# A graph network layer: own rows recomputed in the step loop instead of stored in phase 1, and two parts of a step reordered

## The chip, the cores and the metric

The kernel runs on one core of a Trainium2 chip. The metric is the device time of one execution in microseconds. The engines are PE (TensorE matmuls; PEld its weight loads), DVE (VectorE), ACT (ScalarE), POOL (GpSimd) and SP (SyncE, which here only issues DMAs). Each works through its own list of instructions in order; they meet at semaphores.

## The reference

```python
h = jnp.maximum(_layernorm(x, axis=-1), 0.0)          # x: 6250 x 128
src_h = h[src]                                        # 206250 edges, sorted by dst
parts = [relu(h)]
for t in range(3):
    msg = relu(src_h @ W_e[t].T + b_e[t])             # masked to edge_type == t
    parts.append(segment_sum(msg, dst, num_segments=N))
agg = concatenate(parts, axis=1)                      # 6250 x 512
for t in range(3):
    updated = where(node_type == t, agg @ W_n[t].T + b_n[t], updated)
x = x + updated + h
```

## The kernel before

Nodes stand in 49 blocks of 128 (`NB`). **Phase 1** makes a table of messages in DRAM: for each block ACT normalises x to h (`norm`, L680), PE transposes h (`tr`, L500), ACT copies hT out of PSUM (`copy_t`, L688), PE multiplies hT with the edge weights (`mm`, L506 and L508), ACT or DVE applies relu, and SP stores the rows. Besides, SP stores each hT to `own_hT` (L368), POOL adds h to x in place (L448), and SP stores that in four parts to `own_x` (L372). DVE works on the edges' indices meanwhile.

**The step loop** has 271 steps (`STEPS`). The sorted edges are 403 groups of 512. The first 265 groups (`NS`) are gathered one in each step: POOL fetches message rows by four indirect DMAs (L457), DVE makes a one-hot (`hot`, L973), PE multiplies (`gathered`, L561), DVE adds the sums into `acc` (`add`, L985). The other 138 groups go through counts: they form 23 batches (`BATCHES`) of 6 groups, taken once for each of three edge types, so 69 in all (index q). For each group and type there is a build (`count`, L575): DVE makes two kinds of one-hots (`dense_hot`, L1001 and L1003, at most three sets ahead), PE multiplies them, ACT copies the counts out (`counted`, L743). Seven products (`product`, L589) multiply a batch's counts with message planes held in SBUF. Builds and products are the pieces of a step, three or four, dealt out evenly by `pieces(s)`. A batch ends so: if its last product is in step LAST, then DVE sums three parts in step LAST+1 (`dense_sum`, L1018), PE transposes the slots in LAST+2 (`turn_slots`, L596), and DVE adds six windows into `acc` in LAST+3 (`dense_add`, also L985). The first product of batch q waits for the adds of batch q-2 (L585), because they read the PSUM bank it writes. When the message planes change type, at steps 0 to 3, 86 to 89 and 171 to 175, ACT and DVE split new planes (L752, L754, L1025, L1027).

A node block whose edges are all in is finished (`fin_at`, 49 of them, at least two steps apart and closer together towards the end): SP has loaded `own_x` to `xr` and `own_hT` to SBUF, PE runs L605, L606 (with hT) and L608 into PSUM bank `psF`, DVE adds the masked result to `xr` by three operations (L1036), and SP stores.

DVE's order in a step is: `hot` of the next step, `add`, `dense_add`, `finish`, `dense_hot` for the next step's builds, splits, `dense_sum`. PE's is: `gathered`, `finish`, all pieces, `turn_slots`. ACT's is `counted`, then splits.

Of the kernel before, what the change touches and what calls it, by code (L numbers as in the profile page):

```python
# [4 lines left out]
F32 = mybir.dt.float32  # L5
# [7 lines left out]
P = 128  # L13
# [28 lines left out]
def build(nc, x, src, dst, etype, ntype, w_e, b_e, w_n, b_n, out):  # L42
# [25 lines left out]

    own_x = nc.dram_tensor("own_x", [NB * P, D], F32, kind="Internal").ap()
    own_hT = nc.dram_tensor("own_hT", [NB, D, P], F32, kind="Internal").ap()  # L70
# [68 lines left out]
    with ExitStack() as ctx:  # L139
# [81 lines left out]
        hT_own = work[:, 4 * TD + 4 * D:4 * TD + 8 * D].rearrange("p (s d) -> p s d", s=4)  # L221
        fb_h_own = work[:, 0:D]
        fb_hT_own = work[:, D:2 * D]
# [66 lines left out]
        xh_ok = sem("xh_ok")  # L290
        xh_out = sem("xh_out")
        hT_out = [sem(f"hT_out{i}") for i in range(UN)]
        hT_ld = [sem(f"hT_ld{i}") for i in range(4)]
# [32 lines left out]
        KEPT = (0, 13, 26, 38, NB)  # L326
# [19 lines left out]
        def _(sp):  # L346
# [19 lines left out]
            for i in range(NB):  # L366
                sp.wait_ge(hT_ok, i + 1)
                sp.dma_start(own_hT[i, :, :], hT[:, i % UN, :]).then_inc(hT_out[i % UN], 16)  # L368
                if i + 1 in KEPT:
                    a = KEPT[KEPT.index(i + 1) - 1]  # L370
                    sp.wait_ge(xh_ok, i + 1)
                    sp.dma_start(own_x[a * P:(i + 1) * P, :].rearrange("(b p) d -> p b d", p=P),  # L372
                                 xb[:, a * D:(i + 1) * D].rearrange("p (b d) -> p b d", d=D)).then_inc(xh_out, 16)
                sp.wait_ge(tab_msg[i % UN], i // UN + 1)
                n = min(P, N - i * P)
                sp.dma_start(table[i * P:i * P + n, :], msg[0:n, i % UN, :]).then_inc(tab_out[i % UN], 16)

            for s in range(UN):
                sp.wait_ge(hT_out[s], 16 * len(range(s, NB, UN)))
            sp.wait_ge(xh_out, 16 * (len(KEPT) - 1))  # L380
# [16 lines left out]
            def load_x(j):  # L397
# [4 lines left out]
                sp.dma_start(xr[0:n, j % 4, :], own_x[i * P:i * P + n, :]).then_inc(x_ld[j % 4], 16)  # L402
                sp.dma_start(hT_own[:, j % 4, :], own_hT[i, :, :]).then_inc(hT_ld[j % 4], 16)
# [22 lines left out]
        def _(pool):  # L426
# [18 lines left out]

            for i in range(NB):
                pool.wait_ge(h_ok, i + 1)
                pool.tensor_tensor(xb[:, blk(i)], xb[:, blk(i)], h[:, i % UN, :], ALU.add).then_inc(xh_ok, 1)  # L448
# [34 lines left out]
        def _(pe):  # L483
# [114 lines left out]

            def finish(j):
                i = ORDER[j]  # L600
                pe.wait_ge(hT_ld[j % 4], 16 * (j // 4 + 1))
                if j >= 1:
                    pe.wait_ge(fin_ok, j)
                pe.wait_ge(acc_add, THROUGH[READY[i]])
                pe.matmul(psF[:, 0:TD], ones[:, :], bn_3[:, :], start=True, stop=False)  # L605
                pe.matmul(psF[:, 0:TD], hT_own[:, j % 4, :], wnT[:, 0, :], start=False, stop=False)  # L606
# [7 lines left out]
            for s in range(STEPS):  # L614
                if s < NS:
                    gathered(s)
                for j in fin_at(s - 1):
                    finish(j)
                for kind, i in pieces(s)[:1]:
                    if kind == "build":  # L620
                        count(i)
                    else:
                        product(i)
                for kind, i in pieces(s)[1:]:
# [4 lines left out]
                for q in turns_of(s):  # L629
                    turn_slots(q)  # L630

            rest = pe.value_load(flag[0:1, 0:1], min_val=0, max_val=1)
            with pe.If(rest > 0):
# [11 lines left out]
                with pe.Fori(0, NB) as i:  # L645
                    pe.wait_ge(fb_h, i + 1)
                    pe.transpose(psF[:, TD:TD + P], fb_h_own, ident[:, :]).then_inc(fb_t, 1)
                    pe.wait_ge(fb_hT, i + 1)
                    pe.matmul(psF[:, 0:TD], ones[:, :], bn_3[:, :], start=True, stop=False)
                    pe.matmul(psF[:, 0:TD], fb_hT_own, wnT[:, 0, :], start=False, stop=False)  # L650
# [6 lines left out]
        def _(act):  # L657
# [19 lines left out]
            def norm(i):  # L677
                if i >= UN:
                    act.wait_ge(xh_ok, i - UN + 1)
# [3 lines left out]
            def copy_t(i):  # L683
                act.wait_ge(h_t, i + 1)
                if i >= 4:
                    act.wait_ge(tab_mm, i - 3)
                    act.wait_ge(hT_out[i % UN], 16 * (i // UN))
# [67 lines left out]

            act.wait_ge(xh_out, 16 * (len(KEPT) - 1))
            for s in range(STEPS):
# [377 lines left out]
```

## Time and profile before

| | us |
|---|---|
| three runs | 1755.31, 1756.76, 1765.67 (median 1756.76) |
| the profiled execution, one of the three | 1765.67 |
| its span in the trace | 1763.8 |

In the page, times are microseconds, a line like L589 is line 589 of the kernel, and a group's row gives the mean duration of one instruction and what ended the idle time before it. "issue" as a releaser means that the trace names none on the engine's own side, "remote" one that it does not know. Matmul ends are modelled. Busy time over the span is PE 1514.6 us (86%), DVE 1042.6 (59%), ACT 547.2 (31%), POOL 1163.0 (66%).

### The profile page before, as it was taken

Reading aid. Unit: us, or ns where it says so; the run is one execution under the profiler, and the core shown is the slowest. Engines: PE = TensorE matmul, PEld = TensorE weight load, DVE = VectorE, ACT = ScalarE, POOL = GpSimd, SP = SyncE. Lnnn points to the kernel's source line nnn. Section 1 sums busy time; section 2 is a strip of 40 time slices with the busy share of each in tenths; the row PEclk is TensorE's granted clock in tenths of the full one; section 3 lists DMA queues with packets and bytes.
Section 4 is the critical chain, followed back from the end, with each engine's and each line's share of the span. In section 5 each row is a group of like instructions: output and inputs, shape, how many; then the busy total and the mean of one; then the engine's idle time right before and its main releaser. Section 6 shows DMA issues by size and latency. Waiting matters only on the chain.

```text
span 1763.8 us, 27736 instructions
## 1 busy us (share of the span) xinstructions
PE 1514.6 (86%) x9585; PEld 1191.5 (68%) x9585; DVE 1042.6 (59%) x3461; ACT 547.2 (31%) x1031; POOL 1163.0 (66%) x1125
## 2 busy tenths in 40 slices
PE   6956888988899887889888888887889898989997
PEld 2445677767677676767676777676767777777774
DVE  8565565565656567556555565558556556565642
ACT  7552232322232334322222232234222222223210
POOL 4467666666767676676676677766776666666660
PEclk9868889989999988988988999989999998999998
DMA  8642111111111123111111111213112222122220
GB/s 281 210 123 65 42 48 50 47 49 49 50 49 49 46 68 94 48 49 49 46 47 49 49 47 49 71 47 88 49 50 53 53 53 53 53 58 53 55 54 25
DMA packets 99382, 113.26 MB, mean 64 GB/s; under 512 B 21526, under 2 KB 79413, under 8 KB 99243
## 3 DMA queue, kind: packets, MB, share of 16 engines
q0 software_dynamic: 33920, 69.54, 15.1%
q1 hardware_dynamic: 64445, 40.93, 7.6%
q8 instruction: 78, 1.28, 0.3%
q10 hardware_dynamic: 878, 1.02, 0.2%
q14 instruction: 61, 0.50, 0.1%
HBM read 92.17 MB, written 19.22 MB: 63 GB/s over the span
## 4 chain that ended last, share of the span: by engine, by line
PE 56%; DVE 18%; issue 10%; another core or an unknown queue 10%; ACT 3%; DVEq 2%; DMA 1%; ACTq 0%; SPq 0%
PE ps L589 22%; PE ps L575 13%; PE ps L561 9%; DVE arena L1001 7%; PE ps L608 5%; DVE lhot L1003 4%; DVE acc L985 3%; PE ps L508 2%; PE ps L606 2%; ACT mem L754 1%; DVE xr L1036 1%; DVEq L985 1%; DVE onehot L973 1%; DVE work L1025 1%
## 5 line engine op out<-in xcount | busy, mean ns | idle before, releaser
L457 POOL DMA_INDIRECT rows<-message_table,idx x1060 | 1125.0, 1061 | 515.8 <-issue 284.0
L743 ACT CAST arena<-ps 128x500 f16<-128x500 f32 x828 | 443.0, 581 | 1074.2 <-PE ps L575 636.5
L589 PE MATMUL ps<-mem,arena 128*120 128x384 bf16 x3381 | 698.2, 350 | 42.6 <-issue 35.1
L589 PEld LDWEIGHTS ps<-mem,arena 128*120 128x120 f16 x3381 | 469.6, 145 | 176.2 <-issue 72.0
L575 PE MATMUL ps<-arena,lhot 128*128 128x200 bf16 x3312 | 447.2, 284 | 112.9 <-issue 75.1
L985 DVE TENSOR_TENSOR acc<-ps,acc 128x20 f32 (+1 forms) x679 | 131.7, 194 | 571.3 <-remote 331.0
L1001 DVE TENSOR_SCALAR arena<-iota_j,jkey 128x400 bf16<-128x400 f16 (+1 forms) x1656 | 457.5, 337 | 8.4 <-remote 8.2
L575 PEld LDWEIGHTS ps<-arena,lhot 128*128 128x128 bf16 x3312 | 335.9, 109 | 181.4 <-issue 111.4
L561 PEld LDWEIGHTS ps<-onehot,rows 128*128 128x128 f32 x2120 | 281.5, 202 | 74.1 <-issue 68.6
L561 PE MATMUL ps<-onehot,rows 128*128 128x27 f32 x2120 | 277.4, 270 | 59.4 <-issue 34.3
L1003 DVE TENSOR_TENSOR lhot<-iota_l,lkey 128x512 bf16<-128x512 f16 x414 | 281.2, 679 | 0.0
L608 PE MATMUL ps<-wnT,acc 128*128 128x384 f32 x294 | 117.4, 541 | 0.0
L1036 DVE SCALAR_TENSOR_TENSOR xr<-ps,mask,xr 128x128 f32<-128x128 f32 x147 | 51.5, 351 | 84.1 <-PE ps L608 57.3
L608 PEld LDWEIGHTS ps<-wnT,acc 128*128 128x128 f32 x294 | 62.9, 214 | 47.5 <-issue 15.3
L973 DVE TENSOR_TENSOR onehot<-iota_w,key 128x108 f32<-128x108 f32 x265 | 68.4, 258 | 0.0
L448 POOL TENSOR_TENSOR arena<-arena,work 128x128 f32<-128x128 f32 x49 | 34.3, 710 | 46.3 <-ACT work L680 45.8
L508 PE MATMUL ps<-weT,work 128*128 128x384 f32 x98 | 50.5, 601 | 2.6 <-ACT work L688 2.6
L606 PE MATMUL ps<-wnT,work 128*128 128x384 f32 x98 | 49.5, 590 | 0.3 <-issue 0.3
L1018 DVE TENSOR_REDUCE slots<-ps 120x128 f32<-120x384 f32 x69 | 37.7, 546 | 0.0
L1027 DVE TENSOR_TENSOR mem<-work,mem 128x896 bf16<-128x896 f32 x21 | 22.9, 1092 | 21.1 <-ACT mem L754 19.1
L754 ACT CAST mem<-work 128x896 bf16<-128x896 f32 x21 | 19.7, 938 | 45.9 <-DVE work L1025 29.9
L596 PE MATMUL ps<-ident,slots 120*128 120x120 f32 x69 | 19.2, 279 | 7.6 <-DVE slots L1018 6.5
(105 smaller groups left out, 335.8 us busy)
## 6 DMA issues: line engine op xcount, KB each, us to landing
rows<-message_table,idx POOLq DMA_INDIRECT x1060
message_table<-work SPq DMA_DIRECT2D x48, 192.0 KB, 1.9
work<-message_table SPq DMA_DIRECT2D x18, 448.0 KB
own_hT<-work SPq DMA_DIRECT2D x49, 64.0 KB, 1.7
work<-own_hT SPq DMA_DIRECT2D x49, 64.0 KB
xr<-own_x SPq DMA_DIRECT2D x48, 64.0 KB
out_dram<-xr SPq DMA_DIRECT2D x48, 64.0 KB
own_x<-arena SPq DMA_DIRECT2D x2, 832.0 KB, 4.2
```

What stands on the lines that cost most here:

```text
L457: pool.indirect_dma_start(out=rows[:, g % SLOTS, u, :], out_offset=None, in_=table_rows, in_offset=bass.IndirectOffsetOnAxis(ap=idx[:, g, ...
L508: pe.matmul(psH[s][:, 0:TD], hT[:, s, :], weT[:, :], start=False, stop=True).then_inc(tab_mm, 1)
L561: m = pe.matmul(to[:, :, OFF[u]:OFF[u] + WS], rows[:, s % SLOTS, u, :], onehot[:, s % 4, u, :].rearrange("p (t w) -> p t w", t=T), start=( ...
L575: t = pe.matmul(to[:, :, OFF[u]:OFF[u] + WID[u]], lhot[:, i % HOTS, u, 0:P], jhot[:, i % HOTS, a:a + HH * WID[u]], start=(u == 0), stop=(u ...
L589: m = pe.matmul(psQ[q % 2][0:BG * WG, 0:3 * D], counts[q % 2][:, c * MC + e, :], planes[:, c * MC + e, :, :].rearrange("p v d -> p (v d)") ...
L606: pe.matmul(psF[:, 0:TD], hT_own[:, j % 4, :], wnT[:, 0, :], start=False, stop=False)
L608: m = pe.matmul(psF[:, 0:TD], nodes[:, t, i * P:(i + 1) * P], wnT[:, 1 + t, :], start=False, stop=(t == T - 1))
L743: act.copy(counts[q % 2][:, half * HH:(half + 1) * HH, k * WG:(k + 1) * WG], psB[m % 4][:, 0:HH * WG].rearrange("p (h w) -> p h w", w=WG)) ...
L973: dve.tensor_tensor(onehot[:, s % 4, :, :], iota_b, key[:, s, :].unsqueeze(2).to_broadcast(shape), ALU.is_equal).then_inc(hot_ok, 1)
L985: dve.tensor_tensor(there, sums_, there, ALU.add).then_inc(acc_add, 1)
L1001: dve.tensor_scalar(jhot[:, i % HOTS, JAT[u]:JAT[u] + HB * w], iota_j[w][:, :], float(t * HB * w), jkey[:, g, u:u + 1], ALU.add, ALU.is_equal)
L1003: dve.tensor_tensor(lhot[:, i % HOTS, :, :], iota_l[:, :].unsqueeze(1).to_broadcast([P, TPG, P]), lkey[:, g, :].unsqueeze(2).to_broadcast( ...
```

## The change

- The DRAM buffers `own_x` and `own_hT`, their stores by SP, the add on POOL and all waits for them go.
- In the loop SP loads x itself to `xr`. At the end of the step before a block's step s = FIN, ACT computes h from it (`own_norm`). In step s PE transposes it after the gathered group and ahead of the pieces (`own_transpose`), ACT copies it out of PSUM as the first thing of the step (`own_copy`), and DVE adds h to `xr` (`own`) before `finish` and the one-hots. The block's matmuls follow in step s + 1 as before.
- `turn_slots` moves on PE from the end of a step to behind its first piece.
- `dense_add` moves on DVE from behind `add` to the end of the step.

The core of the diff (left out: the semaphores' names, the views of `work`, and the part that runs only when edges do not fit the plan, which does not happen here):

```diff
@@ sync
             for i in range(NB):
-                sp.wait_ge(hT_ok, i + 1)
-                sp.dma_start(own_hT[i, :, :], hT[:, i % UN, :]).then_inc(hT_out[i % UN], 16)
-                if i + 1 in KEPT:
-                    a = KEPT[KEPT.index(i + 1) - 1]
-                    sp.wait_ge(xh_ok, i + 1)
-                    sp.dma_start(own_x[a * P:(i + 1) * P, :].rearrange("(b p) d -> p b d", p=P),
-                                 xb[:, a * D:(i + 1) * D].rearrange("p (b d) -> p b d", d=D)).then_inc(xh_out, 16)
                 sp.wait_ge(tab_msg[i % UN], i // UN + 1)
...
-            for s in range(UN):
-                sp.wait_ge(hT_out[s], 16 * len(range(s, NB, UN)))
-            sp.wait_ge(xh_out, 16 * (len(KEPT) - 1))
...
-                sp.dma_start(xr[0:n, j % 4, :], own_x[i * P:i * P + n, :]).then_inc(x_ld[j % 4], 16)
-                sp.dma_start(hT_own[:, j % 4, :], own_hT[i, :, :]).then_inc(hT_ld[j % 4], 16)
+                sp.dma_start(xr[0:n, j % 4, :], x[i * P:i * P + n, :]).then_inc(x_ld[j % 4], 16)
@@ gpsimd
-            for i in range(NB):
-                pool.wait_ge(h_ok, i + 1)
-                pool.tensor_tensor(xb[:, blk(i)], xb[:, blk(i)], h[:, i % UN, :], ALU.add).then_inc(xh_ok, 1)
@@ tensor
+            def own_transpose(j):
+                pe.wait_ge(own_h, j + 1)
+                if j >= 1:
+                    pe.wait_ge(fin_ok, j)
+                pe.transpose(psF[:, TD:TD + P], h_own[:, j % 2, :], ident[:, :]).then_inc(own_t, 1)
+
             def finish(j):
                 i = ORDER[j]
-                pe.wait_ge(hT_ld[j % 4], 16 * (j // 4 + 1))
-                if j >= 1:
-                    pe.wait_ge(fin_ok, j)
+                pe.wait_ge(own_st, j + 1)
                 pe.wait_ge(acc_add, THROUGH[READY[i]])
...
-                pe.matmul(psF[:, 0:TD], hT_own[:, j % 4, :], wnT[:, 0, :], start=False, stop=False)
+                pe.matmul(psF[:, 0:TD], hT_own[:, j % 2, :], wnT[:, 0, :], start=False, stop=False)
...
                     finish(j)
+                for j in fin_at(s):
+                    own_transpose(j)
                 for kind, i in pieces(s)[:1]:
                     if kind == "build":
                         count(i)
                     else:
                         product(i)
+                for q in turns_of(s):
+                    turn_slots(q)
                 for kind, i in pieces(s)[1:]:
                     if kind == "build":
                         count(i)
                     else:
                         product(i)
-                for q in turns_of(s):
-                    turn_slots(q)
@@ scalar
             def norm(i):
-                if i >= UN:
-                    act.wait_ge(xh_ok, i - UN + 1)
...
                     act.wait_ge(tab_mm, i - 3)
-                    act.wait_ge(hT_out[i % UN], 16 * (i // UN))
...
-            act.wait_ge(xh_out, 16 * (len(KEPT) - 1))
+            def own_norm(j):
+                i = ORDER[j]
+                act.wait_ge(x_ld[j % 4], 16 * (j // 4 + 1))
+                if j >= 2:
+                    act.wait_ge(own_t, j - 1)
+                    act.wait_ge(own_add, j - 1)
+                act.activation(h_own[:, j % 2, :], xr[:, j % 4, :], ACT.Relu, scale=rstd[:, i:i + 1],
+                               bias=nbias[:, i:i + 1]).then_inc(own_h, 1)
+
+            def own_copy(j):
+                act.wait_ge(own_t, j + 1)
+                if j >= 2:
+                    act.wait_ge(fin_mm, j - 1)
+                act.copy(hT_own[:, j % 2, :], psF[:, TD:TD + P]).then_inc(own_st, 1)
+
             for s in range(STEPS):
+                for j in fin_at(s):
+                    own_copy(j)
                 for kind, i in pieces(s):
                     if kind == "build":
                         counted(i)
                 for m in splits_at(s):
                     split(m)
+                for j in fin_at(s + 1):
+                    own_norm(j)
@@ vector
+            def own(j):
+                dve.wait_ge(own_h, j + 1)
+                dve.tensor_tensor(xr[:, j % 4, :], xr[:, j % 4, :], h_own[:, j % 2, :], ALU.add).then_inc(own_add, 1)
...
-                dve.wait_ge(x_ld[j % 4], 16 * (j // 4 + 1))
+                dve.wait_ge(own_add, j + 1)
...
-            dve.wait_ge(xh_out, 16 * (len(KEPT) - 1))
...
-                for q in adds_of(s):
-                    dense_add(q)
+                for j in fin_at(s):
+                    own(j)
                 for j in fin_at(s - 1):
                     finish(j)
...
                 for q in sums_of(s):
                     dense_sum(q)
+                for q in adds_of(s):
+                    dense_add(q)
```

## Rows read from the trace of the kernel before

**Rows 1.** Page, part 2: TensorE clock in 40 slices, tenths of full speed.

```profile
PEclk9868889989999988988988999989999998999998
```

**Rows 2.** Windows view, three stages: length, busy us (instructions) of PE, PEld, DVE, ACT, POOL, clock.

```profile
0.00:105.00 105.00, 80.78 (x262) 36.69 (x262) 71.54 (x189) 67.61 (x162) 44.70 (x72) 0.92 0.69 228
...
195.00:1715.00 1520.00, 1338.37 (x8839) 1083.31 (x8839) 906.91 (x3084) 448.01 (x818) 1043.85 (x987) 0.92 0.20 53
1715.00:1764.00 49.00, 37.18 (x139) 23.58 (x137) 11.51 (x45) 0.00 (x0) 7.54 (x8) 0.82 0.10 27
```

**Rows 3.** Waits view, 195 to 1715 us: total us, times, longest us.

```profile
DVE acc L985 <- remote: 317.6, 93, 9.4
...
PE ps L575 <- issue: 71.2, 97, 3.2
...
PE ps L575 <- DVE lhot L1003: 25.8, 22, 3.3
```

**Rows 4.** Timeline of 800 to 809 us, DVE, then PE: start, length.

```profile
801.90 0.22 DVE L985 TENSOR_TENSOR acc<-ps,acc 128x60 f32 x1 [1.05 <-PE ps L561]
802.78 0.83 DVE L985 TENSOR_TENSOR acc<-ps,acc 128x20 f32 x3 [0.65 <-issue]
...
804.86 1.12 DVE L1001 TENSOR_SCALAR arena<-iota_j,jkey 128x400 bf16<-128x400 f16 x4
805.90 0.68 DVE L1003 TENSOR_TENSOR lhot<-iota_l,lkey 128x512 bf16<-128x512 f16 x1
...
807.56 0.68 DVE L1003 TENSOR_TENSOR lhot<-iota_l,lkey 128x512 bf16<-128x512 f16 x1
...
804.61 0.97 PE L561 MATMUL ps<-onehot,rows 128*128 128x27 f32 x8
806.64 0.98 PE L575 MATMUL ps<-arena,lhot 128*128 128x200 bf16 x8 [1.06 <-DVE lhot L1003]
807.45 1.15 PE L589 MATMUL ps<-mem,arena 128*120 128x384 bf16 x6
```

**Rows 5.** Timeline: slots' sum and PE's second piece, first and last case.

```profile
245.79 0.55 DVE L1018 TENSOR_REDUCE slots<-ps 120x128 f32<-120x384 f32 x1
...
245.40 1.31 PE L589 MATMUL ps<-mem,arena 128*120 128x384 bf16 x7
...
1625.16 0.55 DVE L1018 TENSOR_REDUCE slots<-ps 120x128 f32<-120x384 f32 x1
...
1625.23 2.13 PE L589 MATMUL ps<-mem,arena 128*120 128x384 bf16 x7
```

**Rows 6.** Groups by line, whole run: busy us, mean ns | idle before, releasers.

```profile
L680 ACT ACTIVATE work<-arena,nbias,rstd 128x128 f32<-128x128 f32 x49 | 23.8, 488 | 0.0
...
L596 PE MATMUL ps<-ident,slots 120*128 120x120 f32 x69 | 19.2, 279 | 7.6 <-DVE slots L1018 6.5 <-issue 1.0
...
L500 PE MATMUL ps<-ident,work 128*128 128x128 f32 x49 | 14.9, 307 | 0.8 <-ACT work L680 0.8
L688 ACT COPY work<-ps 128x128 f32<-128x128 f32 x49 | 12.7, 260 | 7.9 <-DMA own_hT<-work 4.3 <-PE ps L500 2.8 <-PE ps L508 0.7
```

**Rows 7.** Chain that ended last, 54 to 72 us: start, us, what.

```profile
54.74 3.79 DMA own_hT<-work
...
60.23 1.58 PE ps L508 x2
...
62.46 1.58 PE ps L508 x2
...
69.12 1.50 PE ps L508 x2
70.62 0.11 PE ps L500
...
71.00 0.84 PE ps L508 x2
```

**Rows 8.** Timeline of the last two blocks, PE and DVE.

```profile
1753.00 0.32 PE L605 MATMUL ps<-bn,ones 3*128 3x384 bf16 x1 [1.33 <-issue]
...
1757.43 0.32 PE L605 MATMUL ps<-bn,ones 3*128 3x384 bf16 x1 [1.33 <-issue]
...
1756.20 1.12 DVE L1036 SCALAR_TENSOR_TENSOR xr<-ps,mask,xr 128x128 f32<-128x128 f32 x3 [3.30 <-PE ps L608]
```

More of the change, by code:

```diff
@@ L67, in build @@
     table_rows = table.rearrange("n (t d) -> (n t) d", t=T)
-    own_x = nc.dram_tensor("own_x", [NB * P, D], F32, kind="Internal").ap()
-    own_hT = nc.dram_tensor("own_hT", [NB, D, P], F32, kind="Internal").ap()
     D0, D1 = 1, NS - 8
@@ L220, in build @@
         st = [work[:, a * MC * D:(a + 1) * MC * D].rearrange("p (h d) -> p h d", h=MC) for a in range(2)]
-        hT_own = work[:, 4 * TD + 4 * D:4 * TD + 8 * D].rearrange("p (s d) -> p s d", s=4)
-        fb_h_own = work[:, 0:D]
-        fb_hT_own = work[:, D:2 * D]
+        h_own = work[:, 4 * TD + 4 * D:4 * TD + 6 * D].rearrange("p (s d) -> p s d", s=2)
+        hT_own = work[:, 4 * TD + 6 * D:4 * TD + 8 * D].rearrange("p (s d) -> p s d", s=2)
         xr = sb("xr", [P, 4, D])
@@ L289, in build @@
         o_st = [sem(f"o_st{i}") for i in range(4)]
[L290 to L293, printed above, removed]
+        own_h = sem("own_h")
+        own_add = sem("own_add")
+        own_t = sem("own_t")
+        own_st = sem("own_st")
         fin_mm = sem("fin_mm")
@@ L325, in build @@
         SETS = "AAADDDADAD"
-        KEPT = (0, 13, 26, 38, NB)
         EDGE_LOADS = 3 * (GB + 1) + 1
@@ L618, in _ @@
                     finish(j)
+                for j in fin_at(s):
+                    own_transpose(j)
                 for kind, i in pieces(s)[:1]:
[L620 to L624, printed above, removed]
                     if kind == "build":
@@ L630, in _ @@
                     turn_slots(q)
+                for kind, i in pieces(s)[1:]:
+                    if kind == "build":
+                        count(i)
+                    else:
+                        product(i)
             rest = pe.value_load(flag[0:1, 0:1], min_val=0, max_val=1)
@@ L646, in _ @@
                     pe.wait_ge(fb_h, i + 1)
-                    pe.transpose(psF[:, TD:TD + P], fb_h_own, ident[:, :]).then_inc(fb_t, 1)
+                    pe.transpose(psF[:, TD:TD + P], h_own[:, 0, :], ident[:, :]).then_inc(fb_t, 1)
                     pe.wait_ge(fb_hT, i + 1)
                     pe.matmul(psF[:, 0:TD], ones[:, :], bn_3[:, :], start=True, stop=False)
-                    pe.matmul(psF[:, 0:TD], fb_hT_own, wnT[:, 0, :], start=False, stop=False)
+                    pe.matmul(psF[:, 0:TD], hT_own[:, 0, :], wnT[:, 0, :], start=False, stop=False)
                     for t in range(T):
@@ L787, in again @@
                     act.wait_ge(fb_x, i * 16 + 16)
-                    act.activation(fb_h_own, xr[:, 0, :], ACT.Relu, scale=rstd[:, bass.ds(i, 1)],
+                    act.activation(h_own[:, 0, :], xr[:, 0, :], ACT.Relu, scale=rstd[:, bass.ds(i, 1)],
                                    bias=nbias[:, bass.ds(i, 1)]).then_inc(fb_h, 1)
@@ L791, in again @@
                     act.wait_ge(fb_t, i + 1)
-                    act.copy(fb_hT_own, psF[:, TD:TD + P]).then_inc(fb_hT, 1)
+                    act.copy(hT_own[:, 0, :], psF[:, TD:TD + P]).then_inc(fb_hT, 1)
                     act.wait_ge(fb_row, i + 2)
@@ L1103, in _ @@
                     dve.wait_ge(fb_h, i + 1)
-                    dve.tensor_tensor(xr[:, 0, :], xr[:, 0, :], fb_h_own, ALU.add).then_inc(fb_xh, 1)
+                    dve.tensor_tensor(xr[:, 0, :], xr[:, 0, :], h_own[:, 0, :], ALU.add).then_inc(fb_xh, 1)
                     dve.wait_ge(fb_xh, i + 1)
```

## The prediction

> **What bounds the kernel now.** I read the page's clock line first, then the busy time by stage, then who waits for whom inside the long stage, then single stretches in order of time, and last the chain in the first stage and the end. The stages [rows 2] show where the time is: 105 us of preparation, then the step loop, 1520 us of it between 195 and 1715, then 49 us of tail. In the loop PE is busy 1338 of 1520 us, DVE 907, ACT 448, POOL 1044: PE sets the pace, and what can be won or lost is its idle time (182 us), its amount of work, and its clock. The granted clock is 0.92 on the mean there [rows 2]; it goes up and down between slices [rows 1], so some stretches run at the lower of the two levels (1.2 instead of 2.4 GHz), and each hole in PE's work can buy another one.
>
> The waits of the loop [rows 3] say what the holes are: before a build matmul (L575) PE waits 25.8 us, 22 times, for DVE's one-hots (L1003), and 71.2 us over which the trace names no releaser. DVE in turn waits 317.6 us before its add (L985) with an unnamed releaser. So the two engines hand a step back and forth, and the place of DVE's dense add in a step matters, as does every wait that is put in PE's queue.
>
> **Phase 1: the copies of own x and hT go.** PE's chain per tile is two L508, one L500, one L506. At 54.7 us the chain runs over the DMA of own_hT for 3.79 us, and then PE's pair takes 1.58 us instead of 0.84, from 60.23 to 69.12 us, five tiles at the lower clock [rows 7]. Without these 53 stores the table's stores (three times the bytes of hT's) have the DMA queues to themselves. ACT's wait for these stores is 4.3 us in all [rows 6], of which I take 2.5, and I take the slow stretch as its consequence: five tiles at 2.23 us (62.46 less 60.23 is such a distance; the chain's rows are a tile apart) against 1.21 us, 5 x 1.0 = 5.0 us. Sum -7.5 us; bounds 0 (DVE's edge preparation is late by itself) and -9.3 us. The adds on POOL (L448) stand nowhere in that chain; taking them away is worth nothing. SP's queue only becomes shorter.
>
> **The dense add moves behind the one-hots.** In the step at 801 us [rows 4] DVE adds the gathered sums at 801.90, then the six dense adds run from 802.78 to 804.86, and only then come the one-hots of the next step: the first set is ready at 806.58. PE's gathered group ends at 805.59 (804.61 + 0.98), and it waits 1.06 us. With the dense adds last, the first set would be ready about 2.8 us earlier, and this wait goes. But 0.8 us later, at 807.45, PE starts the first product of a batch, and this product waits for the dense adds of the batch before the last (acc_add). In the new order they end where now the second one-hot ends, 807.56 + 0.68 = 808.24: the product starts 0.8 us later than now. The wait is exchanged, not removed. By the plan in the code, 48 of the 67 such products fall into the step right after a dense add; in 18 of them only one piece is ahead, and in 10 two pieces with two sets of one-hots in DVE's way. So up to 28 x 0.8 = 22 us are lost; PE often arrives later than in this row, so I take half, +10. The gain is at most all that [rows 3] name, 25.8, and a part of the unnamed 71.2; it is kept where no product is gated in that step. I take -18: of the 25.8 about half, and 5 us of the unnamed. Net -8 us, bounds -61 (all the named, half the unnamed, no loss) and +22.
>
> **The turn of a batch's slots moves ahead.** PE's L596 needs DVE's sum (L1018). Now it stands last in its step, and waits three times, 6.5 us in all [rows 6]. In the new place it comes after one piece. In the rows, the sum ends at 246.34 where PE passes that place at 245.40, and at 1625.71 against 1625.23 [rows 5]; these are the first and the last of 28 cases (of 68) in which the sum is later, by 30 us together, three of them (the steps of the split planes, 15 us) with a wait already there. While PE waits for the turn, the pieces behind it stand, and with them the next gathered group. But PE's records may run ahead of what it has finished (the unnamed waits of DVE), and then the turn costs nothing. Bounds 0 and +30; I take the middle, +16 us.
>
> **Own h is computed in the loop.** 49 transposes of 128x128 are added to PE. The same form takes 307 ns (L500) and 279 ns (L596) by itself [rows 6], and in a full queue the next matmul starts 0.11 us on, the length of L500 in the chain [rows 7]. 49 x 0.11 = 5.4 to 49 x 0.31 = 15 us; taken 10. TensorE: Matmul & The Clock Gate of the Trainium skill (Part 4, PE-mode transpose) gives about 275 ns for such a transpose inside a kernel; by the page the sum would be 49 x 0.275 = 13.5 us instead of 10, and the forecast 3.5 us higher. The transposes wait for ACT's norm (L680, 488 ns), issued after ACT's copies of the step before; PE has the gathered group (0.98 us) as cover. A copy of a build just ended and the norm are longer than that by 0.1 to 0.5 us where the step ends with a build. Queued behind the waiting transpose are PE's pieces. Bounds 0 and 49 x 0.49 = 24 us; taken +5. ACT's copy (260 ns) and norm are work for an engine that is busy 448 of 1520 us. DVE's added 49 adds of 128x128 have no row; between 0.19 and 0.35 us each they lie in its idle time. SP's load of hT goes, and x is loaded from the input: no change.
>
> **Tail.** At the end a block takes 4.43 us (1753.00 to 1757.43): PE's matmuls, then three DVE operations, and PE starts 0.11 us after DVE ends (1756.20 + 1.12 against 1757.43) [rows 8]. The transpose of a block waits for the end of the block before, so 0.31 + 0.26 + two handovers of 0.1 come on top: 0.75 us x 6 blocks = +4 us; bounds 0 and +6.
>
> **Clock.** More short holes in PE cost clock. I add +3 us (three stretches like that of [rows 7], 1 us each); bounds 0 and +30: at 0.90 instead of 0.92 the 1338 us of PE's work become 1338 x 0.92/0.90 = 1368.
>
> **Sum.** -7.5 - 8 + 16 + 10 + 5 + 4 + 3 = +22.5 us on a span of 1763.8. The profiled execution took 1765.67 us in its own timing, the slowest of the three, the median is 1756.76; 22.5/1765.67 = 1.3%, so 1779 us against the median.
>
> **Rivals.**
> *The new waits are hidden.* PE's finished work lags behind its records, so that turn and norm are there in time: 0 for both, 5 for the transposes, no clock term. -7.5 - 8 + 5 + 4 = -6.5 us: 1750 us. For it: DVE's 317.6 us of unnamed waits [rows 3]; against it: where PE runs without holes (244 to 248 us), the turn's data are late by the records [rows 5].
> *The other side: DVE's order was the main brake.* If the unnamed waits before L575 are in truth late one-hots, half of them goes with the named: -61 + 10 for the gated products, -9 in phase 1, +5 turn, +5, +4: -46 us, 1711 us. It decides the sign of the case as soon as some 40 us of L575's 97 us of idle vanish. Against it: the exchange in [rows 4], and that the new order delays the dense adds for the next products.
> *The clock falls.* The transposes and holes push the granted clock of the loop to 0.90: +22.5 - 3 + 30 = +49.5 us, 1806 us. For it: 0.82 in the tail, where PE's work has such holes already [rows 2].
>
> **How the numbers follow.** Forecast 0.42, hidden waits 0.32, other side 0.14, clock 0.12. About 1% (17.6 us) is what a measurement of this kernel can tell from no change. The forecast's own range is 1764 to 1797, so some of it falls within 1%: slower by over 1% 0.48, within 1% 0.38, faster by over 1% 0.14. The range reaches to the hidden case and a little below it (1743) and up to the clock case (1810), leaving out the other side and the far end of the clock.
>
> **What would show it.** Right: PE's first gathered group some 7 us earlier; L575's wait for L1003 under 12 us; a new wait of L589 for DVE's add of about 10 us; L596's wait for L1018 15 us or more over some 25 places; a tail 4 us longer. Wrong: L596's wait still about 6 us and no wait before the new transposes (hidden case); PE's idle time in the loop down by 40 us (other side); a clock of 0.90 or less, or one above 0.93, in the loop.

## The result, and the profile after

The changed kernel takes 1806.16 us (median of four, 1801.04 to 1811.46) where the kernel before takes 1756.03 (four, 1751.76 to 1765.67): ratio 1.0277, 95% interval [1.0226, 1.0331], slower by about 49 us (1756.03 x 0.0277). Ratios, here and below, leave out executions that took over 1.5% longer than the fastest of the same kernel (three of ten of one kernel below, and one of the kernel before). 1779 us were predicted, with 1743 to 1810 as the range. The direction and the range hold; the size doesn't: +1.3% was forecast, +2.8% came.

The profiled execution took 1800.96 us, 35.3 more than that of before (1765.67, the slowest of its four). Lines have moved: `gathered` is L541 now, `count` L555, `product` L569, `turn_slots` L576, the new transpose L583, PE's `finish` L589 to L592, ACT's `counted` L726, `own_norm` L745, `own_copy` L752, DVE's `add` and `dense_add` L986, the one-hots L1002 and L1004, `dense_sum` L1019, `own` L1032, `finish` L1041.

The page's busy line and clock line of the changed kernel, to be held against [rows 1]:

```profile
PE 1524.0 (85%) x9634; PEld 1201.8 (67%) x9634; DVE 1050.5 (58%) x3510; ACT 579.9 (32%) x1129; POOL 1127.5 (63%) x1076
...
PEclk9977889899989888989888998988899899999997
```

PE is busy 1524.0 us where it was 1514.6: 9.4 us more. The span is 35.1 us longer (1798.9 against 1763.8), so 25.7 us are new idle time of PE. In these two executions most of the cost is waits, not PE's added work.

The windows view, same stages as [rows 2] (the tail is shifted by the 35 us):

```profile
0.00:105.00 105.00, 84.56 (x262) 37.55 (x262) 66.77 (x186) 65.09 (x161) 9.57 (x22) 1.00 0.46 161
195.00:1715.00 1520.00, 1314.10 (x8726) 1069.26 (x8724) 906.11 (x3090) 470.60 (x891) 1025.24 (x970) 0.91 0.19 51
1750.00:1799.00 49.00, 35.97 (x109) 21.31 (x109) 11.93 (x48) 3.56 (x11) 3.38 (x4) 0.74 0.07 18
```

In the same 1520 us of the loop PE gets through 8726 matmuls instead of 8839 and stands idle 206 us instead of 182. The granted clock is 0.91 instead of 0.92. The first stage reads 1.00 (0.92 before) and holds exactly as many matmuls, 262; these two clock figures are too high, as the part on phase 1 shows.

The waits view from 195 to 1715 us (columns as in [rows 3]):

```profile
DVE acc L986 <- remote: 284.6, 93, 7.9
...
PE ps L569 <- issue: 54.1, 80, 8.1
...
PE ps L583 <- ACT work L745: 45.3, 17, 5.3
...
PE ps L555 <- issue: 29.1, 59, 1.4
...
PE ps L576 <- DVE slots L1019: 23.4, 17, 6.5
...
PE ps L569 <- DVE acc L986: 10.2, 10, 2.0
...
PE ps L555 <- DVE lhot L1004: 1.5, 4, 0.6
```

The wait for the one-hots, 25.8 us in [rows 3], is down to 1.5. The turn's wait (L576) has gone from 6.5 us in [rows 6] to 23.4, and the gated product (L569 for L986) has appeared with 10.2. Of the named waits of PE the largest is the one I had costed at 5 us: the new transpose waits 45.3 us, 17 times, for ACT's norm. One of these waits in the timeline of the changed kernel (start, length, engine, line; idle before in brackets):

```profile
1449.43 0.98 PE L541 MATMUL ps<-onehot,rows 128*128 128x27 f32 x8
...
1453.66 1.05 ACT L726 CAST arena<-ps 128x500 f16<-128x500 f32 x2 [2.38 <-remote]
1454.00 0.22 DVE L986 TENSOR_TENSOR acc<-ps,acc 128x60 f32 x1 [2.68 <-remote]
1454.60 0.51 ACT L745 ACTIVATE work<-xr,nbias,rstd 128x128 f32<-128x128 f32 x1
...
1455.16 0.47 PE L583 MATMUL ps<-ident,work 128*128 128x128 f32 x1 [4.75 <-ACT work L745]
```

PE's gathered group ends at 1450.41 by its record, but DVE can add its sums only at 1454.00, and ACT gets the last build of the step before only at 1453.66. (A build's counts come out in two copies.) Behind these two copies stands the norm (1454.60), and behind the norm PE. So of the 4.75 us named, PE has lost about the 1.16 us after 1454.00, and the handover to DVE just before it; earlier its own work wasn't finished. Perfetto Trace Analysis of the Trainium skill (Tensor Engine Instruction) says that a matmul's end in a profile is estimated, not observed. The trace agrees: 3.59 us lie between the recorded end, 1450.41, and the first use of the result, 1454.00.

### The profile page after: what moved, and what is told of

It is laid out like the page before. It is cut to its first block, busy times and chain, and to the rows that moved or that the text cites. A ratio compares the mean times of both kernels' runs of the same rounds, so it can differ in the third digit from the quotient of the medians.

```text
span 1798.9 us, 27966 instructions
## 1 busy us (share of the span) xinstructions
PE 1524.0 (85%) x9634; PEld 1201.8 (67%) x9634; DVE 1050.5 (58%) x3510; ACT 579.9 (32%) x1129; POOL 1127.5 (63%) x1076
## 4 chain that ended last, share of the span: by engine, by line
PE 60%; DVE 14%; issue 11%; another core or an unknown queue 9%; ACT 4%; DVEq 1%; ACTq 0%
PE ps L569 24%; PE ps L555 15%; PE ps L541 8%; DVE arena L1002 5%; PE ps L592 4%; DVE lhot L1004 3%; PE ps L488 3%; DVE acc L986 2%; PE ps L590 2%; ACT arena L726 2%; DVE xr L1041 1%; DVE work L1026 1%; ACT mem L737 1%; PE ps L486 1%
## 5 line engine op out<-in xcount | busy, mean ns | idle before, releaser
L726 ACT CAST arena<-ps 128x500 f16<-128x500 f32 x828 | 446.0, 580 | 1010.4 <-PE ps L555 552.4
L569 PE MATMUL ps<-mem,arena 128*120 128x384 bf16 x3381 | 702.3, 351 | 69.7 <-issue 55.5
L569 PEld LDWEIGHTS ps<-mem,arena 128*120 128x120 f16 x3381 | 472.7, 145 | 200.4 <-issue 98.2
L555 PE MATMUL ps<-arena,lhot 128*128 128x200 bf16 x3312 | 452.4, 288 | 45.9 <-issue 32.2
L1002 DVE TENSOR_SCALAR arena<-iota_j,jkey 128x400 bf16<-128x400 f16 (+1 forms) x1656 | 460.8, 339 | 4.9 <-remote 4.8
L986 DVE TENSOR_TENSOR acc<-ps,acc 128x20 f32 (+1 forms) x679 | 131.4, 193 | 564.8 <-remote 304.7
L555 PEld LDWEIGHTS ps<-arena,lhot 128*128 128x128 bf16 x3312 | 346.6, 111 | 109.8 <-issue 67.1
L541 PEld LDWEIGHTS ps<-onehot,rows 128*128 128x128 f32 x2120 | 282.5, 201 | 62.1 <-issue 57.0
L541 PE MATMUL ps<-onehot,rows 128*128 128x27 f32 x2120 | 275.7, 269 | 52.2 <-issue 32.8
L1004 DVE TENSOR_TENSOR lhot<-iota_l,lkey 128x512 bf16<-128x512 f16 x414 | 281.1, 679 | 0.0
L1041 DVE SCALAR_TENSOR_TENSOR xr<-ps,mask,xr 128x128 f32<-128x128 f32 x147 | 51.5, 350 | 103.3 <-PE ps L592 71.8
L592 PE MATMUL ps<-wnT,acc 128*128 128x384 f32 x294 | 109.0, 508 | 0.6 <-issue 0.5
L592 PEld LDWEIGHTS ps<-wnT,acc 128*128 128x128 f32 x294 | 58.3, 199 | 43.0 <-issue 6.8
L583 PE MATMUL ps<-ident,work 128*128 128x128 f32 x49 | 16.9, 345 | 58.4 <-ACT work L745 45.3
L488 PE MATMUL ps<-weT,work 128*128 128x384 f32 x98 | 55.0, 649 | 0.0
L752 ACT COPY work<-ps 128x128 f32<-128x128 f32 x49 | 13.0, 266 | 120.7 <-PE ps L583 72.3
L583 PEld LDWEIGHTS ps<-ident,work 128*128 128x128 f32 x49 | 8.9, 182 | 64.3 <-ACT work L745 47.5
L576 PE MATMUL ps<-ident,slots 120*128 120x120 f32 x69 | 21.1, 305 | 26.7 <-DVE slots L1019 23.4
L1019 DVE TENSOR_REDUCE slots<-ps 120x128 f32<-120x384 f32 x69 | 37.7, 546 | 0.0
```

Of the source, the lines that this page charges most:

```text
L488: pe.matmul(psH[s][:, 0:TD], hT[:, s, :], weT[:, :], start=False, stop=True).then_inc(tab_mm, 1)
L541: m = pe.matmul(to[:, :, OFF[u]:OFF[u] + WS], rows[:, s % SLOTS, u, :], onehot[:, s % 4, u, :].rearrange("p (t w) -> p t w", t=T), start=( ...
L555: t = pe.matmul(to[:, :, OFF[u]:OFF[u] + WID[u]], lhot[:, i % HOTS, u, 0:P], jhot[:, i % HOTS, a:a + HH * WID[u]], start=(u == 0), stop=(u ...
L569: m = pe.matmul(psQ[q % 2][0:BG * WG, 0:3 * D], counts[q % 2][:, c * MC + e, :], planes[:, c * MC + e, :, :].rearrange("p v d -> p (v d)") ...
L592: m = pe.matmul(psF[:, 0:TD], nodes[:, t, i * P:(i + 1) * P], wnT[:, 1 + t, :], start=False, stop=(t == T - 1))
L726: act.copy(counts[q % 2][:, half * HH:(half + 1) * HH, k * WG:(k + 1) * WG], psB[m % 4][:, 0:HH * WG].rearrange("p (h w) -> p h w", w=WG)) ...
```

## The parts one by one

The moves can be made without the rest, and the rest without the moves. All ratios below are against runs of the kernel before on the same chip, whose medians there were 1741.93 to 1747.31 us; 0.1% is 1.75 us. The runs stand on four chips. Two ratios of different chips can differ by more than their intervals say: one kernel was taken on two of them and gave 0.9904 and 0.9975 (phase 1, below).

**The turn early, alone:**

```diff
                 for kind, i in pieces(s)[:1]: ...
+                for q in turns_of(s):
+                    turn_slots(q)
                 for kind, i in pieces(s)[1:]: ...
-                for q in turns_of(s):
-                    turn_slots(q)
```

> The kernel before with one part of the change alone: the turn of the slots moved on PE from the end of a step to behind its first piece. Theory (the turn is a cost of its own): the trace of the changed kernel has PE waiting 23.4 us at L576 for DVE's sum, against 6.5 us before, so +15 to +25 us (1.009 to 1.014). Rival (PE's work is behind its records, the wait is hidden, and the loss comes from the own part): within 5 us of before, 0.997 to 1.003. In the profile the transpose of the slots should wait some 20 us or more for the sum in the one, and about 6 in the other.

Measured 1.0064 [1.0026, 1.0102], some 11 us, less than expected and more than the rival. Its waits view, same stretch:

```profile
PE ps L596 <- DVE slots L1018: 37.5, 23, 8.4
```

The wait is new at this size, and costs less than it names.

**The dense add late, alone:**

```diff
-                for q in adds_of(s):
-                    dense_add(q)
...
                 for q in sums_of(s):
                     dense_sum(q)
+                for q in adds_of(s):
+                    dense_add(q)
```

> The kernel before with one part of the change alone: DVE's dense add moved to the end of its step. Theory: the waits of the builds for the one-hots (25.8 us) mostly go and products wait about 10 us for the adds; the steps behind a dense add get shorter, so -10 to -30 us (0.983 to 0.994). Rival 1 (exchange only): 0.997 to 1.003. Rival 2 (the late adds hold up the products more than they give): 1.005 or more.

Measured 1.0036 [1.0008, 1.0064]: a loss of 6 us where the prediction had a gain of 8. Its waits view:

```profile
PE ps L589 <- DVE acc L985: 17.7, 19, 2.4
...
PE ps L575 <- DVE lhot L1003: 5.1, 10, 0.8
```

The builds wait 20.7 us less for the one-hots (5.1 against 25.8 in [rows 3]), the products 17.7 us more for the adds. By the names that is even; by the measured time it is a loss.

**Both moves:**

> The kernel before with both moves, turn early and dense add late, and the own rows still stored in phase 1. If the two are independent, the sum of the two runs with one move each: by the theory -10 to +10 us, 0.994 to 1.006, so that nearly all of the loss of 2.8% is the own part's. Rival (the moves together are the loss): 1.015 or more.

Measured 1.0091 [1.0052, 1.013]: they add up (0.64 + 0.36 = 1.0%).

**The own part alone** (the change without the two moves):

> The kernel before with the third part alone: own x and hT no longer stored in phase 1 but computed in the step loop, the order of turn and dense add as before. Theory (the wait of the new transpose for ACT's norm, 45.3 us over 17 waits in the trace of the changed kernel, is real): +35 to +55 us, 1.020 to 1.031. Rival (that wait is the time in which PE works off what its records ran ahead): +10 to +20 us, 1.006 to 1.012.

Measured 1.015 [1.0081, 1.0219] over four runs, 26 us, about half of the loss, and between the two expectations. Its waits view:

```profile
PE ps L583 <- ACT work L745: 42.3, 17, 8.4
```

Own part and both moves give 2.4% of the 2.8%, within the intervals all of it.

## The own part taken apart

**The norm two steps ahead.** Here ACT computes h behind the copies of the step before the last, so that it is there long before PE asks:

```diff
-                for j in fin_at(s + 1):
+                for j in fin_at(s + 2):
                     own_norm(j)
```

> The own part alone (as in the run e4_own, 1.015), with one thing changed: ACT issues a block's norm at the end of the step two before the transpose, not one before. Theory (the loop's loss in the own part is PE's wait for the norm, 42.3 us over 17 waits in that run's trace): the wait falls under 5 us and most of the loss goes, ratio 0.997 to 1.004. Rival (the wait stands where PE works off its backlog, and the loss is the work added to PE, ACT and DVE): the wait is gone from the rows and the ratio stays at 1.012 to 1.018.

Measured 1.0023 [0.9986, 1.0059] against 1.015: by this, the one line is worth 22 us. The same line in the changed kernel with both moves:

> The changed kernel with one thing undone: the norm is issued two steps ahead of the transpose, not one. Theory (the wait for the norm costs 1.3% wherever turn and dense add stand, and the parts add up): 1.0277 less 0.013, so 1.010 to 1.018. Rival (the parts are not independent, the turn's wait takes over): 1.022 or more.

Measured 1.012 [1.008, 1.016] against 1.0277, 27 us. The transpose's row in the groups by line, first the changed kernel, then the one with the line changed (busy us, mean ns, idle before and its releasers):

```profile
L583 PE MATMUL ps<-ident,work 128*128 128x128 f32 x49 | 16.9, 345 | 58.4 <-ACT work L745 45.3 <-DVE xr L1041 5.3 <-issue 4.5
```

```profile
L583 PE MATMUL ps<-ident,work 128*128 128x128 f32 x49 | 15.3, 312 | 5.3 <-DVE xr L1041 5.3
```

The wait is gone from the trace and the time from the measurement, in two kernels. That is shown. The size is less sure: the runs of a pair were not taken together, those of the first pair on two chips, and by the intervals the line is worth 9 to 36 us in the one kernel and 16 to 39 us in the other, in both more than the 5 us of the prediction.

**The transposes alone.** PE gets 49 transposes more, of a tile that is always ready; nothing reads them:

```diff
+                for j in fin_at(s):
+                    if j >= 1:
+                        pe.wait_ge(fin_ok, j)
+                    pe.transpose(psF[:, TD:TD + P], weT[:, 0:P], ident[:, :])
                 for kind, i in pieces(s)[:1]: ...
```

> The kernel before with 49 transposes of 128x128 added on PE at the place where the changed kernel has them, of a constant, with no wait for ACT and no copy, so that nothing uses their result. By the prediction's row +5 to +15 us (1.003 to 1.009); the rival of the own part (the added PE work is the loss) +20 us or more (1.012).

Measured 0.9979 [0.9952, 1.0005]. Their row in the groups by line:

```profile
L622 PE MATMUL ps<-ident,weT 128*128 128x128 f32 x49 | 16.1, 328 | 5.7 <-DVE xr L1040 4.8 <-issue 0.9
```

16.1 us of busy PE, and by the interval at most 0.05% = 0.9 us of time. 10 us was too much; that the cost is under the 5.4 us of the lower bound is less sure, since ratios of one kernel on two chips differed by 0.7%.

**ACT's copy behind the counts' copies** (with the norm two steps ahead):

```diff
-                for j in fin_at(s):
-                    own_copy(j)
                 for kind, i in pieces(s):
                     if kind == "build":
                         counted(i)
+                for j in fin_at(s):
+                    own_copy(j)
```

> The own part alone with the norm two steps early (e5_norm2, 1.0023), and ACT's copy of the transposed h moved from the front of ACT's step to behind the step's copies of counts. Theory (some 20 us of the loop's cost are left once the wait for the norm is gone, and they stand in ACT's queue: ACT waits 27.4 us for the transpose and 51 us for an unnamed releaser at that copy, with the copies of counts queued behind): 0.992 to 0.998. Rival (ACT has the time; the rest is DVE's added work or chance): 1.000 to 1.004.

Measured 1.0144 [1.0079, 1.0209] over five runs where 0.992 to 0.998 was expected, worse by 1.2% than with the copy ahead (by the medians, 1765.19 against 1747.31, the ratio is 1.010, and it is worse by 0.7%). The waits view has a new row, PE's first matmul of `finish` in the next step:

```profile
PE ps L589 <- ACT work L752: 19.9, 14, 4.8
```

It is the norm's mistake over again: in these 14 steps what ACT does behind the copies of a step comes after PE's gathered group of the next. The copy has to stay ahead of them.

**Without DVE's adds of h** (a bare semaphore increment in their place, norm two steps ahead; this kernel leaves h out of the residual):

> As e5_norm2, without DVE's added adds of h to x (49 of 282 ns): a bare semaphore increment stands in their place, so h is missing from the residual of the output. Theory (DVE's added work in front of the one-hots is what is left): 0.992 to 0.998. Rival (it lies in DVE's idle time): 1.000 to 1.004.

Measured 0.9985 [0.9952, 1.0017], 0.4% below the kernel with them, some 7 us, with intervals that overlap, so a cost of the adds isn't shown. **The adds at the end of their step,** first with the late copy:

> Own part alone, with all three hidden: the norm two steps early, ACT's copy behind the copies of counts, DVE's add of h at the end of its step. If the loop's cost is queueing only, phase 1's gain (0.990 in the run e7_phase1) remains less some 5 us in the tail: 0.992 to 0.996, faster than both kernels. If the work itself costs: 0.999 to 1.004.

Measured 1.0141 [1.0103, 1.0179], where at most 1.004 was expected: as bad as the late copy by itself (1.0144). Then with the copy in its place:

> The own part with ACT's norm issued two steps ahead (1.0023 alone), and DVE's add of h to xr behind the one-hots and sums of its step instead of ahead of them. Without these adds at all the ratio was 0.9985. If what they cost is their place ahead of the one-hots, this kernel takes 0.999; if it is the finish waiting for them, or DVE's time itself, it stays at 1.002 or more. ACT's copy stays first in its step, since moving it behind the counts' copies made PE's finish wait for it (43 us in all before the first matmul of the finish).

Measured 1.0003 [0.997, 1.0036] against 1.0023 with the adds ahead of the one-hots. This is the best the own part has given; it equals the kernel before, and no kernel with all of the reference's work in it was measurably faster.

## Is there anything to gain in the build's wait?

If a late dense add only hurts where a product is gated, it should help when it is made late nowhere else:

```diff
+    def free_late(q):
+        return q + 2 >= NQ or PROD_STEP[(q + 2) * MC] >= LAST[q] + 5
...
                 for q in adds_of(s):
-                    dense_add(q)
+                    if not free_late(q):
+                        dense_add(q)
...
+                for q in adds_of(s):
+                    if free_late(q):
+                        dense_add(q)
```

> The kernel before with the dense add moved to the end of its step only for the 19 of 69 batches after which no product in the next step waits for it (and the last two batches). Theory (moving the add late loses, 1.0036 in the run e2_add, because the first product of a batch then waits for it, 17.7 us over 19 waits): here the gain stays and the loss goes, 0.993 to 0.998. Rival (the builds' wait for one-hots was PE's backlog being worked off, so that there is nothing to gain): 0.999 to 1.003.

Measured 0.9997 [0.9965, 1.003]. The waits view (`count` is L578 here, the one-hots L1006):

```profile
PE ps L564 <- DVE acc L988: 30.4, 14, 5.4
PE ps L578 <- DVE lhot L1006: 16.6, 24, 2.1
```

No product waits for an add, the builds wait 9 us less than before by name, and nothing is gained. But only 21 of the 69 adds are late here, and another wait has grown: the gathered group (L564) waits 30.4 us for DVE's adds, where it waits 16.4 us in the kernel before and 9.6 to 24.8 us in the others. So it isn't shown whether the builds' wait holds nothing, or whether what it gives is lost again at the gathered group. That the gate on the products is what makes the late add a loss (1.0036) is argued, not shown: 1.0036 and 0.9997 have intervals that overlap.

## Phase 1

**Without own stores, POOL's adds and their waits,** twice, on two chips (in the loop x is loaded in place of what was stored, so this kernel leaves h out of the residual and multiplies x in place of h; the next two leave out the one or the other):

> The kernel before without its stores of own x and hT and without the add on POOL; the loop's two loads stay, but read x, so the outputs of this kernel lack h in the residual and have x in place of hT. It prices phase 1 alone. Theory (as predicted, and as the run e4_own shows with its first gathered group at 96.9 us): -6 to -10 us, 0.994 to 0.997. Rival (as in the trace of the changed kernel, whose first group starts at 106.8 us, no gain since PE sets the pace): 0.999 to 1.002.

> The kernel before without own stores, POOL's adds and their waits, once more, with x loaded in the loop in place of both (output lacks h, own product wrong). By the first series 0.990 [0.9865, 0.9942]. If that holds, 1727 us or so; if it was scatter, 0.997 or more. Its profile is a second look at when the step loop begins: phase 1's gain shows there as a start before 101 us, a gain of the loop as one at 103 to 105 us with a shorter stretch behind it.

Measured 0.9904 [0.9865, 0.9942] over 6 runs the first time, 0.9975 [0.9946, 1.0004] over 12 the second. The two don't meet: intervals of this size are a little too narrow here. (By the medians, 1731.13 against 1743.63, the first ratio is 0.993.) **Without POOL's adds alone, and without hT's stores alone:**

> The kernel before without POOL's 49 adds of h to x in phase 1 and the waits for them; own_x then holds x, so the output lacks h. All stores and loads stay. Taking stores, adds and their waits away together gave 0.990, but PE's first gathered group began at 104.7 us against 101.2 to 105.6 us in the six kernels that keep them, so it isn't plain that the gain lies in phase 1, nor which of the parts makes it. If the adds hold ACT (its norm waits for them by xh_ok), this kernel takes 1733 us or so (0.994). If they stand on no chain, as the prediction had it, 1.000 +- 0.002.

> The kernel before without the 49 stores of hT and ACT's wait for them; in the loop the same number of bytes is loaded from x in place of hT, so the own product of the output is wrong. own_x and POOL's adds stay. If these stores are what phase 1 waits for (the prediction's term of 7.5 us), 0.996 or less, and with the run without POOL's adds it makes up the 0.990; if both come out at 1.000, the 0.990 lay in the waits together or in what the loop loads.

Measured 0.9964 [0.9935, 0.9994] and 0.9986 [0.9959, 1.0012]. All four say a few us; none says which part it is.

The traces say more. PE's first gathered group in the kernel before, in the changed one, in the own part alone, and in the second run without the stores (timeline rows):

```profile
105.61 1.88 PE L561 MATMUL ps<-onehot,rows 128*128 128x27 f32 x8 [5.66 <-issue]
```

```profile
106.80 1.88 PE L541 MATMUL ps<-onehot,rows 128*128 128x27 f32 x8 [5.44 <-issue]
```

```profile
96.88 1.88 PE L541 MATMUL ps<-onehot,rows 128*128 128x27 f32 x8 [5.45 <-DVE onehot L974]
```

```profile
99.95 1.88 PE L545 MATMUL ps<-onehot,rows 128*128 128x27 f32 x8 [5.45 <-DVE onehot L953]
```

The changed kernel and the own part alone have the same phase 1, and differ by 10 us. The chain that ended last shows why, first in the changed kernel, then in the own part alone (a pair of the table's matmuls each):

```profile
16.49 1.58 PE ps L488 x2
...
43.13 1.58 PE ps L488 x2
...
47.28 0.84 PE ps L488 x2
```

```profile
23.16 1.49 PE ps L488 x2
25.02 0.84 PE ps L488 x2
```

PE starts phase 1 at a slow pace in every execution and goes over to full pace at a moment that is not the kernel's: at 47.2 us in one, at 24.9 in the other. Of the table's matmuls, two to a tile, the first takes 1008 ns at the one pace and 590 at the other, the second 847 and 486, and a tile 2.22 us against 1.22. Two stretches of the kernel before show what pace that is (windows view, L508 alone: length, busy us of PE and PEld, clock):

```profile
16.40:22.60 6.20, 4.94 (x6) 1.50 (x6) 1.00 1.00 333
60.20:70.40 10.20, 7.91 (x10) 2.47 (x10) 0.50 0.44 147
```

In all 18 profiled kernels the first record, at full clock, lies within 0.3 us of the end of the last slow matmul of the start. With the time before it at the lower level, the first 105 us of the kernel before have a clock of 0.81, and those of the changed one 0.78, not 0.92 and 1.00.

Over the 18 profiled kernels, 4 to 28 of the 98 such matmuls are slow, each 0.5 us late. Taking that off, the first gathered group begins at 97.5 us on the mean (95.2 to 100.5) in the six kernels that keep stores and adds, at 95.9 without POOL's adds, at 96.9 without hT's stores, and at 93.5 (92.8 to 95.2) in the ten without both. So phase 1 gains 4 us by its waits, and the start of an execution gives or takes up to 12.

Not all slow matmuls belong to the start. Three of the six kernels that keep stores and adds have a second slow stretch, of 10 (the kernel before), 6 (the transposes alone) and 4 matmuls (the dense add late), and none of the twelve others has one. Each comes after an idle time of PE of 1.7 to 2.3 us that stands behind a store of hT; in the kernel before:

```profile
58.95 0.91 PE L508 MATMUL ps<-weT,work 128*128 128x384 f32 x2 [2.25 <-ACT work L688]
```

The turn alone has the same wait, 2.25 us, and no slow stretch after it. These stretches are worth 20 x 0.5 / 6 = 1.7 us on the mean of the six, so phase 1 gains 4 to 6 us.

## Why the prediction came out as it did

**The norm (term +5, bounds 0 and 24): the step that failed.** I counted a copy and the norm against the whole gathered group as cover (0.98 us), longer "by 0.1 to 0.5 us". It was the cover that failed. In the trace two copies of the step before stand ahead of the norm (1.05 us), PE goes on 1.50 us after they begin, and the gathered sums are there 0.34 us after they begin, not 0.98: about 1.16 us are lost in that place, 1.08 and 1.13 in the ones at 1083.58 and 1363.85 us. Undoing it gave 22 us and 27 us, at 17 named waits some 1.3 to 1.6 us each with what hangs on them. The place and the queue were right, and the upper bound of 24 us lies between the two measurements; the value I took was a quarter of what it was, or less.

**The dense add (term -8): the second step that failed, in its sign.** The exchange was right (12 us or less for L1003's wait: 5.1 and 1.5; about 10 for the product's: 17.7 and 10.2). Wrong was that 18 us of the builds' wait could be had on top of it: alone, the late add gave +6 us [+1, +11] instead of -8. Where the gain went stays open. Either the wait held little: PE's results come some us behind its records (3.59 us above), so that a wait between records can lie where PE is still at work. Or what it gave was lost again elsewhere, as at the gathered group in the kernel with 21 late adds, where 9 us of the builds' wait went, 14 us came there, and the time stayed the same. No run separates the two.

**The turn (term +16, bounds 0 and 30):** 11 us, with 37.5 us over 23 places alone and 23.4 over 17 in the changed kernel. Right in place; in size 5 us high, within the interval (5 to 18 us).

**The transposes (+10, bounds 5.4 and 15):** below both bounds by the interval, at most 0.9 us. The 13.5 us by TensorE: Matmul & The Clock Gate of the Trainium skill (Part 4, PE-mode transpose) would have been further off still; the duration that it states, about 275 ns, in a sentence on bf16, lies near the f32 rows here (269 ns at the least, 328 on the mean). I took a duration as a cost; on this PE the 16.1 us of busy time went for the most part into idle time that was there.

**DVE's added adds (taken at nothing):** 282 ns each, within the range I gave. By the kernel without them they cost some 7 us, 3.5 of them by their place ahead of the one-hots, but both differences are smaller than their intervals: that they cost anything is not shown.

**Phase 1 (-7.5, bounds 0 and -9.3):** the stores' waits gave more than the 2.5 us I took (4 us in the traces). The slow stretch of five tiles in [rows 7], 5 us of the term, is found in no kernel without stores of hT, and so may well be a consequence of them, but only three of the six kernels with stores and adds have one: it is worth 1.7 us on their mean, not 5. Together -5.7 us. The 7 us earlier start wasn't there in the changed kernel (106.80 against 105.61), because its execution ran 28 matmuls slowly, all at the start, against 16.

**The tail (+4, bounds 0 and 6):** right in size, only in part for the reason given. The last block but one of the changed kernel:

```profile
1785.34 0.30 PE L583 MATMUL ps<-ident,work 128*128 128x128 f32 x1 [1.38 <-DVE xr L1041]
1785.68 0.27 ACT L752 COPY work<-ps 128x128 f32<-128x128 f32 x1 [6.03 <-PE ps L583]
1786.00 0.33 PE L589 MATMUL ps<-bn,ones 3*128 3x384 bf16 x1 [0.36 <-ACT work L752]
...
1787.01 3.51 PE L592 MATMUL ps<-wnT,acc 128*128 128x384 f32 x6
```

The same six matmuls in the kernel before:

```profile
1754.00 2.10 PE L608 MATMUL ps<-wnT,acc 128*128 128x384 f32 x6
```

Against [rows 8] the transpose and the copy put 0.66 us (1786.00 less 1785.34) into a block's chain; 0.75 was the estimate. But such a block takes 6.55 us here where it takes 4.43 in [rows 8]: most of the difference is the matmuls at the lower clock (847 ns where 486 stood before; the tail's granted clock is 0.74 against 0.82). In seven of the eight profiled kernels with the own part, part of the last three blocks' matmuls run at this pace, in none of the ten others. From the last gathered group's start to DVE's last operation the eight take 24.7 us on the mean (21.6 to 26.8), the ten 19.5 (17.8 to 20.8): +5 us, of transposes, copies and clock together.

**The clock (+3):** 0.91 in the loop, between the forecast (no change that rows would show) and the clock case (0.90). The other profiled kernels lie between 0.92 and 0.93 there, faster and slower ones alike. Its price in the loop isn't separate from the waits'; the clock case gave 1806 us, which is the measured time, but that is luck: the clock didn't fall to 0.90, the transposes that should have driven it cost nothing that was measured, and one moved line takes back 27 us.

**The sum.** With the measured sizes: phase 1 -6, dense add +6, turn +11, transposes 0, norm +22, DVE's adds +7, tail +5, together +45 of the 49 us. That it comes so close is in part luck: single terms are known to 5 us at best, DVE's adds and the transposes not apart from 0. The forecast's +22.5 lacked 17 us for the norm, 14 for the dense add, 7 for DVE's adds and 2.5 for phase 1 and the tail, and had 10 us too much for the transposes, 5 for the turn and 3 for a clock term that no run shows by itself. The range holds 1806 us only through its clock case, not through the norm or the dense add.

## What to carry to other kernels

Work put at the end of an in-order queue starts when the queue's last input comes, not when the step ends: count everything that stands ahead of it, and give it a whole step of slack where the buffers allow it. A wait's total in a trace is not its cost where the engine's ends are modelled: 42.3 us named for the norm were worth 22, 31 us more for the turn 11, while 19.9 us for the late copy cost about as much as they named. Before counting on one, look at when the engine's results are first used, and when a wait goes, look for the one that grew instead. And when an execution starts with a stretch whose length is chance, compare where it ends, not only when the next stage begins.

## What the hardware showed that I had not expected

PE ran the start of phase 1 at the lower of its two levels (1.2 GHz), 1008 ns for a matmul that takes 590 later, for 4 to 31 us from one execution to the next, though it was busy without a break (30.30 of 30.30 us in the changed kernel). What ends the stretch stays open. The profile's clock figures don't show it: a granted clock of 1.00 at the start of a trace can be the absence of a record, and a matmul whose duration is known from later stretches tells the two apart. The parts are additive to a degree that I had not looked for: moves 0.64 and 0.36 against 0.91 together, own part and moves 2.4 against 2.77.
